# Graph attention on all rows of each head: scores, maxima, exponentials and sums on 128 partitions; logits one step later

## The chip, the cores and the metric

The kernel is one program on one NeuronCore of a Trainium2 chip. The metric is the device time of one execution in microseconds, the median over several runs. "One chunk" below is 512 edges. Engines are named as the profile names them: PE (TensorE), DVE (VectorE), ACT (ScalarE), POOL (GpSimd) and SP (SyncE, which only issues transfers here).

## The reference, cut to what matters

The network takes 100,000 nodes of 64 features and 50,000 edges sorted by destination, and runs four graph layers, each behind a layer norm and a ReLU. Three of the edge passes are attention over the incoming edges of a node, in this form:

```python
z = leaky_relu(xl[src] + xr[dst] + ee, 0.2)          # [E, H, C]
score = einsum('ehc,hc->eh', z, att)                 # one score per edge and head
m = segment_max(score, dst)
a = exp(score - m[dst])
denom = segment_sum(a, dst)
msg = xl[src] * (a / denom[dst])[..., None]
out = segment_sum(msg, dst)
```

Stage a has 8 heads of 16 channels (128 rows), stage b 2 heads of 64 channels (128 rows, and its input has 128 features, so both ends of an edge need a turn of their own), and stage g 4 heads of 16 channels (64 rows). Between b and g stands another layer; its logits are the product of each normalised end of an edge with a weight vector of 64 (`h[src] @ a_src`, `h[dst] @ a_dst`).

## The kernel before, in words

The edges are padded to 98 chunks of 512. `gat_block` is written once and called for stages a, b and g; `R` is the number of feature rows, `H` the number of heads, `wide` is true for b alone. Each engine has its own program, a software pipeline made by `flow` (line 114): a list of stages, each with the number of steps by which it lags, and in step t a stage that lags by s handles chunk t - s. Within a step an engine does its stages in the order of the list, and semaphores tie the engines together. With `SL` = 4 slots, four chunks can be under way in most buffers. A wait on an engine holds everything behind it.

For one chunk, in the order of the data:

- SP loads the indices of both ends (`indices`, line 679), the edge features (`extras`, 690) and START, a row of 512 numbers that is 0 inside a segment and very negative at its start, copied to `H` partitions (`starts`, 704). In stage a SP also stores the gathered rows (693) and the slots that ACT read out of them (697 and 699), behind a wait for `at`; the index loads of a later chunk stand behind these in its queue.
- POOL gathers the rows with eight indirect transfers of 128 rows each (`gather`, 722).
- DVE and ACT normalise in a and g (`norm`, lines 579 to 603; `normed`, 841); in a, ACT then copies two integers out of the gathered rows (`at`, 849).
- PE turns the chunk so that features lie on partitions (`turn`, 929 and 932), ACT copies it (`turned`, 861 and 862), and PE projects it (`project`, 946 to 951) into `bZ` (both ends and the edge) and `bX` (the source alone).
- ACT and DVE make `zt`, the leaky value (`values` 878, `leaky` 760, 761 and 765), and ACT makes `xl` (869 and 871).
- PE makes the scores: `att1b` and its likes are [R, H], so the scores lie on 8, 2 or 4 partitions (`scores`, 957).
- DVE makes the running maximum of a segment with a scan and the two exponents, the decay (row 0) and the weight (row 1) (`maximum`, 774 to 778), and ACT the exponentials `ex` (885).
- DVE scans the denominator on `H` partitions (`denominator`, 787), reading `ex` twice.
- PE spreads decay and weight from H to R rows by products with the 0/1 matrices `sel8`, `sel2` and `sel4` (`factors`, 964 and 965), into the banks `bF0` and `bF1`.
- DVE multiplies weight by `xl` (`sums`, 794) and scans the numerator (799), reading both factors from those banks.
- PE turns numerator (972) and denominator (977, eight small matmul instructions a chunk) so that edges lie on partitions again (`results`). In b, the denominators share the bank `bF2` with the second turn of a later chunk, so there are waits for each other (`rec` in `turn`, `h` in `results`).
- DVE takes the reciprocal (806) and multiplies (812 and 815, 820, or 823), and ACT stores the rows (889).

The list that sets the order on PE is short enough to quote, with that of DVE in stages a and g:

```python
stages = [(L, project), (L + 1, factors), (L, scores), (L - 1, turn), (L + 1, results)]        # PE
stages = [(L, leaky), (L + 2, quotients), (L + 1, denominator), (L + 1, sums), (L, maximum), (L - 2, norm)]
```

`L` is 3 in a and g and 2 in b, which has no norm.

`logit_block` (line 1247) works on 49 batches of 1024 edges with 3 slots: POOL gathers eight times (1290), DVE adds the base rows (1306) and takes the moments, ACT normalises with 16 instructions (1339), and DVE multiplies (1320, two instructions) and sums (1326). On DVE a step is the logits of batch t - 2 and then the norm of t - 1; on ACT it is the stores of the logits of t - 2 and then the normalising of t - 1.

Stage f (`relation_block`, line 1685) is not touched. Its SP queue holds two broadcasts of 256 KB (`kp`, 1746) and 512 KB (`rl`, 1741) ahead of an index load (1731) for which the gathers (1762) wait.

## Time and profile before

| What | us |
|---|---|
| median of 3 runs | 9635.66 (9634.32 to 9646.82) |
| the profiled execution's own time | 9562.17 |
| its span, first to last instruction | 9560.3 |
| DVE busy, share of the span | 6713.4, 70% |
| PE busy | 5960.4, 62% |
| POOL busy | 4490.4, 47% |
| ACT busy | 2831.8, 30% |
| stage a: first and last norm of a gathered row start | 779.8 and 2216.2 |
| stage b: first and last turn start | 2280.8 and 3707.9 |
| logits stage: first and last addition start | 4532.6 and 5266.8 |
| stage g: first and last addition of base rows start | 6991.2 and 8290.4 |

The stages run one after another, so each has its own limit, and the shares of the whole span say little. The lines of an instruction are those of the listing; names such as `a_xg` are the stage's letter and the buffer. PE's bars are modelled, two passes of an f32 product of 512 columns count as two instructions. "issue" as the end of a wait means that the profile shows nothing that the engine waited for. PEclk is the granted clock of TensorE as a share of 2.4 GHz.

### The profile page before, as it was taken

What the parts mean: (1) busy time and instruction counts of PE and PEld (TensorE: products, weight loads), DVE (VectorE), ACT (ScalarE), POOL (GpSimd) and SP (SyncE); (2) the same over time, 40 slices, a digit from 0 to 9 for tenths busy, and PEclk for the clock granted to TensorE, in tenths of its full rate; (3) what the DMA queues carried; (4) which work ended last, traced back from release to release, by engine and by line L of the source; (5) the groups of instructions that cost most, each with busy time, mean ns of one, the idle gap of its engine ahead of it and who ended that gap; (6) DMA issues with size and microseconds to landing.
All of it is one profiled execution on the core that took longest, in us unless ns stands there. A gap on an engine that the chain in (4) does not pass through costs nothing. (4 is left out here: it accounts for less than half of the span.)

```text
span 9560.3 us, 99896 instructions
## 1 busy us (share of the span) xinstructions
PE 5960.4 (62%) x15032; PEld 2923.7 (31%) x15032; DVE 6713.4 (70%) x20701; ACT 2831.8 (30%) x6861; POOL 4490.4 (47%) x4367
## 2 busy tenths in 40 slices
PE   0006999996999997776000889867869999800000
PEld 0002333332444444664000446723323333300000
DVE  2677888885666665887555898867869999877422
ACT  0002333331111112554333000134434444346300
POOL 1775555554555553554554000055556666313466
PEclk9998555555656665555555897578855555555555
DMA  4002334432222221111333002566633333322222
GB/s 146 1 1 44 56 56 56 56 56 50 47 47 47 46 47 28 36 37 44 85 88 80 5 4 67 150 109 130 128 67 74 72 74 73 81 89 110 79 82 78
DMA packets 937356, 627.70 MB, mean 66 GB/s; under 512 B 649081, under 2 KB 811542, under 8 KB 935760
## 3 DMA queue, kind: packets, MB, share of 16 engines
q1 hardware_dynamic: 580324, 305.65, 12.4%
q0 software_dynamic: 137984, 138.92, 11.8%
q10 hardware_dynamic: 218920, 181.82, 5.8%
q14 instruction: 96, 0.79, 0.0%
q8 instruction: 32, 0.52, 0.0%
HBM read 431.25 MB, written 228.04 MB: 69 GB/s over the span
## 5 line engine op out<-in xcount | busy, mean ns | idle before, releaser
L722 POOL DMA_INDIRECT a_xg<-t_XL,a_ix x784 | 785.5, 1002 | 668.3 <-issue 647.5
L722 POOL DMA_INDIRECT b_xg<-t_H,b_ix x784 | 783.3, 999 | 668.1 <-PE b_bank L932 379.6
L722 POOL DMA_INDIRECT g_xg<-t_D,g_ix x784 | 825.8, 1053 | 527.7 <-issue 227.4
L1762 POOL DMA_INDIRECT f_dg<-t_D,f_ix x392 | 383.9, 979 | 1291.1 <-DMA f_ix<-t_PSRC 1163.7
L1105 POOL DMA_INDIRECT t_RANK<-m_place,m_at x392 | 384.5, 981 | 415.0 <-DMA m_place<-t_POS 307.3
L1290 POOL DMA_INDIRECT l_d<-t_D,l_ix x392 | 370.8, 946 | 401.7 <-DVE l_xs L1306 234.1
L2177 POOL DMA_INDIRECT out<-o_y,o_ix x392 | 386.6, 986 | 230.9 <-issue 198.7
L1380 PE MATMUL pr_prow<-c_ident,pr_col 128*1 128x128 f32 x2 | 0.6, 394 | 786.0 <-DVE pr_col L1398 786.0
L445 POOL DMA_INDIRECT t_XL<-ix_pv,ix_si x392 | 407.9, 1041 | 160.0 <-issue 137.7
L760 DVE TENSOR_TENSOR b_zt<-b_xl,b_bank 128x512 f32<-128x512 f32 x98 | 67.4, 687 | 550.9 <-issue 210.2
L1339 ACT ACTIVATE l_hn<-l_xs,l_sm 128x64 f32<-128x64 f32 x784 | 265.0, 426 | 501.7 <-issue 259.6
L2056 POOL TENSOR_TENSOR n_x<-n_x,c_c 128x1280 f32<-128x1280 f32 (+1 forms) x40 | 158.5, 3964 | 513.4 <-DVE n_y L2086 311.0
L1883 ACT ACTIVATE f_hn<-f_xs,f_bykind 128x64 f32<-128x64 f32 x784 | 265.0, 426 | 293.0 <-DVE f_bykind L1793 230.5
L529 PE MATMUL ix_bk<-c_ident,ix_key 128*128 128x128 f32 x56 | 15.6, 435 | 525.0 <-issue 372.9
L2153 DVE TENSOR_TENSOR o_t<-o_ag,c_k 128x256 f32<-128x256 f32 x98 | 41.7, 425 | 416.0 <-DMA o_x<-t_X 330.7
L2099 ACT ACTIVATE n_h<-n_x,n_sm 128x64 f32<-128x64 f32 (+1 forms) x800 | 269.4, 426 | 196.0 <-DVE n_sm L603 196.0
L841 ACT ACTIVATE a_hn<-a_xg,a_sm 128x64 f32<-128x64 f32 x784 | 270.0, 428 | 152.2 <-DVE a_sm L603 106.2
L841 ACT ACTIVATE g_hn<-g_xg,g_sm 128x64 f32<-128x64 f32 x784 | 269.9, 426 | 65.2 <-DVE g_sm L603 59.8
L1128 PE MATMUL m_pa<-c_wca,m_h 65*128 65x64 f32 x784 | 192.7, 427 | 127.4 <-ACT m_h L1209 83.6
L1459 PE MATMUL pb_sums<-pb_rhs,pb_lhs 128*128 128x392 f32 x784 | 260.6, 496 | 12.6 <-DVE pb_rhs L1450 12.6
L1459 PE MATMUL ps_sums<-ps_rhs,ps_lhs 128*128 128x392 f32 x784 | 261.2, 497 | 8.4 <-DVE ps_rhs L1450 8.4
L861 ACT ACTIVATE b_hT<-b_bank 128x512 f32<-128x512 f32 x98 | 58.5, 597 | 673.2 <-PE b_bank L932 640.2
(439 smaller groups left out, 17014.5 us busy)
## 6 DMA issues: line engine op xcount, KB each, us to landing
t_XL<-in_nodes ACTq DMA_DIRECT2D x10, 2578.1 KB
t_XSD<-a_xg SPq DMA_DIRECT2D x98, 256.0 KB
t_H<-a_oE ACTq DMA_DIRECT2D x98, 256.0 KB
l_xb<-t_XSD SPq DMA_DIRECT2D x49, 512.0 KB
f_rl<-t_REL SPq DMA_DIRECT2D x49, 512.0 KB
g_xb<-t_XSD SPq DMA_DIRECT2D x98, 256.0 KB
n_x<-in_x SPq DMA_DIRECT2D x39, 640.0 KB
out<-n_y ACTq DMA_DIRECT2D x39, 640.0 KB
```

The costliest lines, as they stand in the source:

```text
L445: nc.gpsimd.indirect_dma_start(lp, bass.IndirectOffsetOnAxis(ap=si[k][:, j:j + 1], axis=0), pv[k][:, j:j + 1].bitcast(F32), None, bounds_c ...
L722: nc.gpsimd.indirect_dma_start(xg[k][:, j, i, :], None, table, bass.IndirectOffsetOnAxis(ap=ix[k][:, i, j:j + 1], axis=0)).then_inc(s_g[k] ...
L841: last = f(hn[k][:, g // 2, g % 2, :], xg[k][:, g // 2, g % 2, 0:D], ACT.Relu, bias=sm[:, 5, g:g + 1], scale=sm[:, 4, g:g + 1])
L1105: nc.gpsimd.indirect_dma_start(rank, bass.IndirectOffsetOnAxis(ap=at[k][:, j:j + 1], axis=0), place[k][:, j:j + 1], None).then_inc(s_rank[ ...
L1128: last = nc.tensor.matmul(pa[0][k % 2][:, j, :], h[k][:, j * P:(j + 1) * P], C["wca"][:, :], start=True, stop=True)
L1290: nc.gpsimd.indirect_dma_start(d1[k][:, 0, j, :], None, T["D1"], bass.IndirectOffsetOnAxis(ap=ix[k][:, j:j + 1], axis=0)).then_inc(s_g[k], 16)
L1339: last = nc.scalar.activation(hn[k][:, g % 2, g // 2, :], xs[k][:, g // 2, g % 2, :], ACT.Relu, bias=sm[:, 5, g:g + 1], scale=sm[:, 4, g:g ...
L1459: nc.tensor.matmul(sums[:, :], lhs[c % SL][:, :], rhs[c % SL][:, :], start=(c == 0), stop=(c == EF - 1)).then_inc(s_mm, 1)
L1762: nc.gpsimd.indirect_dma_start(dg[k][:, u, j, :], None, T["D2"], bass.IndirectOffsetOnAxis(ap=ix[k][:, u, j:j + 1], axis=0)).then_inc(s_g[ ...
L1883: last = f(hn[k][:, g // J, g % J, c, :], xs[k][:, g // J, g % J, :], ACT.Relu, bias=by_kind[:, c, 1, g:g + 1], scale=by_kind[:, c, 0, g:g ...
L2099: last = f(h[k][0:np_, g, :], x3[k][0:np_, g, :], ACT.Relu, bias=sm[0:np_, 5, g:g + 1], scale=sm[0:np_, 4, g:g + 1])
L2177: nc.gpsimd.indirect_dma_start(out, bass.IndirectOffsetOnAxis(ap=ix[k][:, j:j + 1], axis=0), y[k][:, j, :], None, bounds_check=N - 1, oob_ ...
```

## The change

In the attention stages the attention vectors become [R, 128] matrices in which the column of a head stands once for each row of the head, so that the scores come out on all 128 partitions. Maxima, exponents and exponentials are then made on 128 partitions, START is loaded to 128 partitions, and the products with the 0/1 matrices, the matrices themselves and the banks `bF0` and `bF1` are gone. In a and b the denominator is scanned on 128 rows and turned with four transposes of 128x128 into a bank of its own (`bD`); four numerator transposes stay. In g (`both`), the rows 64 to 127 of the product's operand stay plain weights, the rows 0 to 63 are multiplied in place, and one scan makes numerators and denominators, which are turned together. The second turn of b has its own bank (`bT2`), and its waits on the shared bank go. In `logit_block` there are four slots, and the logits and their stores lag by 3 steps instead of 2.

```diff
@@ setup_block, POOL
-            for name, w in (("sel8", 16), ("sel2", 64), ("sel4", 16)):
...
@@ gat_block
-        start = [m.sb(f"start{k}", [H, CH]) for k in slots]
+        start = [m.sb(f"start{k}", [P, CH]) for k in slots]
...
-        bT, bZ, bX, bS, bF0, bF1, bF2, bO = (m.ps(f"bank{b}", [P, CH]) for b in range(8))
+        bT, bT2, bZ, bX, bS, bD, bO = (m.ps(f"bank{b}", [P, CH]) for b in range(7))
...
-                sp.dma_start(start[k][:, :], line(T["START"], n, H)).then_inc(s_start[k], 16)
+                sp.dma_start(start[k][:, :], line(T["START"], n, P)).then_inc(s_start[k], 16)
...
             def sums(n, k, q, old):
                 ch4.at(n)
-                dve.wait_ge(S["b"], n + 1)
+                dve.wait_ge(S["ex"], n + 1)
                 dve.wait_ge(S["xl"], n + 1)
-                ch4(v.tensor_tensor(msg[:, :], bF1[0:R, :], xl[k][:, :], ALU.mult))
                 if later(n):
                     dve.wait_ge(S["sum"], n)
+                weighted = ex[k][0:R, 1, :] if both else msg[:, :]
+                ch4(v.tensor_tensor(weighted, ex[k][0:R, 1, :], xl[k][:, :], ALU.mult))
                 if old:
                     dve.wait_ge(S["o"], n - SL + 1)
-                v.tensor_tensor_scan(num[k][:, :], bF0[0:R, :], msg[:, :], num[(k - 1) % SL][:, CH - 1:CH],
-                                     ALU.mult, ALU.add).then_inc(S["sum"], 1)
+                v.tensor_tensor_scan(num[k][:, :], ex[k][:, 0, :], ex[k][:, 1, :] if both else msg[:, :],
+                                     num[(k - 1) % SL][:, CH - 1:CH], ALU.mult, ALU.add).then_inc(S["sum"], 1)
...
-                stages = [(L, leaky), (L + 2, quotients), (L + 1, denominator), (L + 1, sums), (L, maximum), (L - 2, norm)]
+                stages = [(L, leaky), (L + 2, quotients), (L + 1, sums), (L, maximum), (L - 2, norm)]
+                if not both:
+                    stages.insert(2, (L + 1, denominator))
...
             def exponents(n, k, q, old):
...
-                    act.wait_ge(S["b"], n - SL + 1)
-                    act.wait_ge(S["den"], n - SL + 1)
+                    act.wait_ge(S["sum"], n - SL + 1)
+                    if not both:
+                        act.wait_ge(S["den"], n - SL + 1)
...
-                if wide and later(n, 3):
-                    pe.wait_ge(S["rec"], n - 2)
...
-                mm(bS[0:H, :], att[:, :], zt[k][:, :], start=True, stop=True).then_inc(S["s"], 1)
-
-            def factors(n, k, q, old):
-
-                pe.wait_ge(S["ex"], n + 1)
-                if later(n):
-                    pe.wait_ge(S["sum"], n)
-                mm(bF0[0:R, :], sel[:, :], ex[k][:, 0, :], start=True, stop=True)
-                mm(bF1[0:R, :], sel[:, :], ex[k][:, 1, :], start=True, stop=True).then_inc(S["b"], 1)
+                mm(bS[:, :], att[:, :], zt[k][:, :], start=True, stop=True).then_inc(S["s"], 1)
...
                 for j in range(J):
-                    tr(bO[:, j * R:(j + 1) * R], split(num[k][:, :])[:, :, j], C["ident"][0:R, 0:R])
-                if wide:
-
-                    hold(pe, S["pturn"], (S["h"], min(n + 3, NCH) if isinstance(n, int) else n + 3))
-                for j in range(J):
-                    last = mm(bF2[:, j * H:(j + 1) * H], split(den[k][:, :])[:, :, j], C["ident"][0:H, 0:H],
-                              start=True, stop=True)
+                    last = tr(bO[:, j * P:(j + 1) * P], split(num[k][:, :])[:, :, j], C["ident"][:, :])
+                    if not both:
+                        last = tr(bD[:, j * P:(j + 1) * P], split(den[k][:, :])[:, :, j], C["ident"][:, :])
                 last.then_inc(S["o"], 1)
-            stages = [(L, project), (L + 1, factors), (L, scores), (L - 1, turn), (L + 1, results)]
+            stages = [(L, project), (L, scores), (L - 1, turn), (L + 1, results)]
@@ weights_block, DVE
+            for name, heads, again in (("att1", 8, 1), ("att2", 2, 1), ("att3", 4, 2)):
...
+                    v.tensor_copy(C[name + "r"][:, :].rearrange("p (g h c) -> p g h c", g=again, c=width)[:, g, :, :],
+                                  bcast(att[:, :], width))
@@ logit_block
-        SL = 3
+        SL = 4
...
-            flow(dve, [(2, logits), (1, norm)], total=NB, slots=SL)
+            flow(dve, [(3, logits), (1, norm)], total=NB, slots=SL)
...
-            flow(act, [(2, store), (1, normed)], total=NB, slots=SL)
+            flow(act, [(3, store), (1, normed)], total=NB, slots=SL)
```

## Rows read from the trace of the kernel before

**Rows 1.** Windows of a, b, g: length, PE, PEld, DVE, ACT, POOL busy us, PEclk, DMA share, GB/s.

```profile
900.00:2200.00 1300.00, 1219.93 (x2370) 501.54 (x2370) 1044.87 (x3228) 502.98 (x1220) 702.00 (x700) 0.52 0.39 56
2400.00:3600.00 1200.00, 1134.82 (x2576) 528.83 (x2576) 741.35 (x1080) 227.88 (x333) 666.55 (x666) 0.61 0.23 47
7100.00:8200.00 1100.00, 1092.10 (x2178) 421.28 (x2178) 1017.25 (x3166) 470.62 (x1000) 707.57 (x668) 0.50 0.36 74
```

**Rows 2.** Timeline, stage a: start us, us, engine, line, instruction [idle before <-releaser].

```profile
1217.47 1.11 DVE L579 BATCH_NORM_STATS2 a_bn<-a_xg 128x6 f32<-128x64 f32 x8 [3.32 <-DMA a_xg<-t_XL,a_ix]
...
1224.90 0.20 ACT L849 ACTIVATE a_at<-a_xg 128x8 int32<-128x8 int32 x1
...
1229.81 0.37 SPq L679 DMA_DIRECT2D a_ix<-t_DST  x1
...
1233.12 0.94 POOL L722 DMA_INDIRECT a_xg<-t_XL,a_ix  x1 [5.88 <-issue]
...
1246.36 0.73 DVE L579 BATCH_NORM_STATS2 a_bn<-a_xg 128x6 f32<-128x64 f32 x5 [2.05 <-DMA a_xg<-t_XL,a_ix]
```

**Rows 3.** Waits of VectorE in stage a, 900 to 2200: total us, times, longest.

```profile
DVE a_bn L579 <- DMA a_xg<-t_XL,a_ix: 162.5, 77, 3.6
```

**Rows 4.** Timeline, stage b, one cycle.

```profile
2861.93 0.69 DVE L760 TENSOR_TENSOR b_zt<-b_xl,b_bank 128x512 f32<-128x512 f32 x1 [4.94 <-issue]
...
2866.55 1.28 DVE L799 TENSOR_TENSOR_SCAN b_num<-b_bank,b_num,b_msg 128x512 f32<-128x512 f32 x1
...
2868.30 1.08 PE L972 MATMUL b_bank<-c_ident,b_num 128*128 128x128 f32 x4
...
2869.85 1.99 PE L977 MATMUL b_bank<-c_ident,b_den 2*128 2x2 f32 x8 [0.47 <-ACT b_hT L862]
...
2871.77 1.13 PE L949 MATMUL b_bank<-b_hT,c_wr 128*128 128x512 f32 x2
...
2873.29 2.08 PE L951 MATMUL b_bank<-b_hT,c_wl 128*128 128x512 f32 x2
...
2876.12 0.69 DVE L760 TENSOR_TENSOR b_zt<-b_xl,b_bank 128x512 f32<-128x512 f32 x1 [4.93 <-PE b_bank L951]
```

**Rows 5.** Waits of VectorE in stage g, 7100 to 8200, the largest.

```profile
DVE g_zt L765 <- issue: 7.4, 20, 1.6
```

**Rows 6.** Timeline, logits stage, one cycle.

```profile
4813.98 1.29 DVE L1320 TENSOR_TENSOR l_pr<-l_hn,c_wb 128x512 f32<-128x512 f32 x2 [5.64 <-issue]
...
4818.48 0.94 POOL L1290 DMA_INDIRECT l_d<-t_D,l_ix  x1 [5.36 <-DVE l_xs L1306]
...
4828.98 1.29 DVE L1320 TENSOR_TENSOR l_pr<-l_hn,c_wb 128x512 f32<-128x512 f32 x2 [5.62 <-issue]
```

**Rows 7.** Timeline, stages a and g: gathers beside VectorE instructions.

```profile
1223.98 1.26 DVE L787 TENSOR_TENSOR_SCAN a_den<-a_ex,a_den 8x512 f32<-8x512 f32 x1
1224.32 1.68 POOL L722 DMA_INDIRECT a_xg<-t_XL,a_ix  x1 [0.30 <-issue]
...
1225.86 1.28 DVE L799 TENSOR_TENSOR_SCAN a_num<-a_bank,a_num,a_msg 128x512 f32<-128x512 f32 x1
...
1226.30 0.94 POOL L722 DMA_INDIRECT a_xg<-t_XL,a_ix  x1 [0.31 <-issue]
...
8132.46 0.67 DVE L777 TENSOR_TENSOR g_rp<-g_r,g_start 4x512 f32<-4x512 f32 x1
...
8132.53 1.41 POOL L722 DMA_INDIRECT g_xg<-t_D,g_ix  x1 [0.30 <-issue]
```

**Rows 8.** Timeline, stage f: an index load behind two broadcasts.

```profile
6513.47 0.53 SPq L1746 DMA_DIRECT2D f_kp<-t_KEEP  x1
...
6514.27 0.35 SPq L1741 DMA_DIRECT2D f_rl<-t_REL  x1
...
6515.01 0.19 SPq L1731 DMA_DIRECT2D f_ix<-t_PSRC  x1
...
6521.14 0.94 POOL L1762 DMA_INDIRECT f_dg<-t_D,f_ix  x1 [3.75 <-DMA f_ix<-t_PSRC]
```

More of the change, by code:

```diff
@@ L633, in gat_block @@
         xl = [m.sb(f"xl{k}", [R, CH]) for k in slots]
-        r = [m.sb(f"r{k}", [H, CH + 1]) for k in slots]
-        ed = [m.sb(f"ed{k}", [H, 2, CH]) for k in slots]
-        ex = [m.sb(f"ex{k}", [H, 2, CH]) for k in slots]
-        rp = m.sb("rp", [H, CH])
-        den = [m.sb(f"den{k}", [H, CH]) for k in slots]
-        recT = [m.sb(f"recT{k}", [P, J * H]) for k in slots]
+        r = [m.sb(f"r{k}", [P, CH + 1]) for k in slots]
+        ed = [m.sb(f"ed{k}", [P, 2, CH]) for k in slots]
+        ex = [m.sb(f"ex{k}", [P, 2, CH]) for k in slots]
+        rp = m.sb("rp", [P, CH])
+        both = R < P
+        if not both:
+            den = [m.sb(f"den{k}", [P, CH]) for k in slots]
+        recT = [m.sb(f"recT{k}", [P, J, H]) for k in slots]
         msg = m.sb("msg", [R, CH])
-        num = [m.sb(f"num{k}", [R, CH]) for k in slots]
+        num = [m.sb(f"num{k}", [P, CH]) for k in slots]
         if wide:
@@ L804, in quotients @@
                 dve.wait_ge(S["o"], n + 1)
-                v.reciprocal(recT[k][:, :], bF2[:, 0:J * H]).then_inc(S["rec"], 1)
+                weights = (bO if both else bD)[:, :].rearrange("p (j r) -> p j r", j=J)[:, :, (R if both else 0)::R // H]
+                v.reciprocal(recT[k][:, :, :], weights).then_inc(S["rec"], 1)
                 dve.wait_ge(S["rec"], n + 1)
@@ L860, in turned @@
                 if wide:
-                    f(hT2[k][:, :], bF2[:, :], ACT.Copy)
+                    f(hT2[k][:, :], bT2[:, :], ACT.Copy)
                 f(hT[k][:, :], bT[:, :], ACT.Copy).then_inc(S["h"], 1)
@@ L882, in exponents @@
                 if old:
-                    act.wait_ge(S["b"], n - SL + 1)
-                    act.wait_ge(S["den"], n - SL + 1)
+                    act.wait_ge(S["sum"], n - SL + 1)
+                    if not both:
+                        act.wait_ge(S["den"], n - SL + 1)
                 f(ex[k][:, :, :], ed[k][:, :, :], ACT.Exp).then_inc(S["ex"], 1)
@@ L956, in scores @@
                     hold(pe, S["pturn"], (S["ed"], n))
-                mm(bS[0:H, :], att[:, :], zt[k][:, :], start=True, stop=True).then_inc(S["s"], 1)
-            def factors(n, k, q, old):
-                pe.wait_ge(S["ex"], n + 1)
-                if later(n):
-                    pe.wait_ge(S["sum"], n)
-                mm(bF0[0:R, :], sel[:, :], ex[k][:, 0, :], start=True, stop=True)
-                mm(bF1[0:R, :], sel[:, :], ex[k][:, 1, :], start=True, stop=True).then_inc(S["b"], 1)
+                mm(bS[:, :], att[:, :], zt[k][:, :], start=True, stop=True).then_inc(S["s"], 1)
             def results(n, k, q, old):
-                hold(pe, S["pturn"], (S["sum"], n + 1), (S["den"], n + 1))
+                hold(pe, S["pturn"], (S["sum"], n + 1))
+                if not both:
+                    hold(pe, S["pturn"], (S["den"], n + 1))
                 if later(n):
@@ L1026, in _ @@
             three_parts(nc, ch, wrow, parts, rest)
+            for name, heads, again in (("att1", 8, 1), ("att2", 2, 1), ("att3", 4, 2)):
+                att = C[name + "b"]
+                rows_ = att.shape[0]
+                width = P // (heads * again)
+                for g in range(again):
+                    v.tensor_copy(C[name + "r"][:, :].rearrange("p (g h c) -> p g h c", g=again, c=width)[:, g, :, :],
+                                  bcast(att[:, :], width))
             for q in range(2):
@@ L1317, in logits @@
                 dve.wait_ge(s_hn, n + 1)
+                if later(n):
+                    dve.wait_ge(s_e, n)
                 for i in range(2):
```

44 lines of the change are left out of this document (19 added, 25 removed).

## The prediction

> **What bounds the kernel now.** I read the busy shares of three attention stages first, then one cycle of each in order of time, and asked which wait ends last. The shares mislead: TensorE is busy 94%, 95% and 99% of the stretches of stages a, b and g [rows 1], yet only in two of them would less TensorE work help at once. Each chunk has eight gathers, so their count gives the pitch of a chunk: 700 in 1300 us is 14.86 us in a, 666 in 1200 us is 14.41 us in b, 668 in 1100 us is 13.17 us in g [rows 1].
>
> Stage a turns on a loop over two chunks without TensorE. Norm of a chunk starts at 1217.47, its slots (`at`) are out on ACT at 1225.10, SP stores them and only then loads the indices of the chunk two ahead (DST issued 1229.81), its first gather starts at 1233.12, and the norm that waited for it starts at 1246.36 [rows 2]: 28.9 us here, 2 x 14.86 = 29.7 in the mean. VectorE waited for these gathers 77 times in 87 chunks [rows 3].
>
> Stage b turns on a loop through PE, ACT and VectorE: leaky starts at 2861.93, the numerator scan ends at 2867.83, four transposes (1.08 us) start at 2868.30, the eight small denominator matmuls (1.99 us) wait 0.47 us for ACT and start at 2869.85, projection starts at 2871.77, and leaky of the next chunk at 2876.12 [rows 4]. 14.19 us.
>
> Stage g has both engines full: PE 1092 of 1100 us, and the largest wait on VectorE is 7.4 us in 84 chunks [rows 1, 5]; its 13.17 us are VectorE's instructions with the semaphore steps between them.
>
> The logits stage repeats every 15.00 us and VectorE stands 5.6 us of it waiting for the 16 normalising activations of the same batch; the gathers idle 5.36 us [rows 6].
>
> **The change, part by part.** *Stage g.* VectorE loses the denominator scan: 1.26 us (the same scan lasts that in a [rows 7]); scan and product keep their length, since 4, 8 and 128 rows of one width cost the same (1.26 us on 8 rows, 1.28 on 128 [rows 7]). PE loses two factor products and eight small matmuls and is no longer full. Gathers need 707.57/83.5 = 8.47 us busy plus 8 x 0.30 us steps = 10.9 us a chunk [rows 1], below 13.17 - 1.26 = 11.9, so VectorE stays the bound: -1.26 x 98 = **-123 us**. Ends: -60 if gathers or ACT start to interfere, -123 as VectorE loses no more.
>
> *Stage b.* VectorE keeps every instruction from leaky to numerator scan, 5.90 us. Then, 0.1 us later as a semaphore step, eight 128x128 transposes, 2 x 1.08 = 2.16 us; the turn that stands before them now runs earlier, because the factor products (L964, L965) are gone. The small matmuls' wait for ACT goes with the shared bank, so nothing stands between. Projection to leaky 4.35 us as now. 5.90 + 0.1 + 2.16 + 4.35 = 12.5 against 14.19: -1.68 x 98 = **-165 us**. Scores with 128 weight columns may take 2.08 us, as L951 does; they lie beside VectorE's quotients and scans. The gathers' own 666.55/83.25 + 2.4 = 10.4 us stay below. The unknown is the clock. In this cycle L949 took 1.13 us for its two passes and L951 2.08 [rows 4]; the first ran at the 2.4 GHz level, the second at 1.2; the stretch's granted clock is 0.61, that of g 0.50, the lower level throughout [rows 1]. With both slow the gain is 0.73 us a chunk, -72 us; with both fast 2.63, -258 us. I take today's mix, the nearest row. The exponential's new wait (for the numerator scan four chunks back) is long past when it is reached.
>
> *Stage a.* TensorE's relief is worth nothing on the loop. Two things are added to it. First, message product and numerator scan read SBUF on both sides instead of one PSUM side. A gather that started 0.34 us into the denominator scan (both inputs in SBUF) lasted 1.68 us and ended 0.76 us after the scan did; one that started 0.44 us into the numerator scan (one input in PSUM) took 0.94 us [rows 7]. So a run of D us of such instructions delays the gather that starts s us into it by D - 0.17 - s: for D = 1.26 that is 0.47 us in the mean over a pitch of 1.25 us, for denominator scan plus product (1.92 us) 1.12. The product's result must be waited for before the scan, and in such a gap a waiting gather gets in: one that started 0.07 us into L777 ended 1.41 us later, not after L778 [rows 7]. The numerator scan then holds the next one 0.07 us. Together +0.7 us a group. Second, START grows from 16 KB to 256 KB (128 copies of one line) and stands in SP's queue just ahead of the index loads that the loop waits for. In stage f an index load issued right behind broadcasts of 256 and 512 KB was used 6.13 us after its issue [rows 8], in a 3.31 us after [rows 2]: 2.8 us for 768 KB, 0.93 for 256 KB; bounds 0 (hidden) and 2.8. So (0.7 + 0.93)/2 x 98 = **+80 us**, ends 0 and +230. The same START in b and g meets index loads that are chunks ahead: nothing, and if that cover were gone, 0.9 us a chunk. VectorE's 1044.87 of 1300 us leaves room for the norm to start when data lands.
>
> The Trainium skill ("SBUF — State Buffer", Who interferes with whom) holds that a tensor_tensor with two SBUF inputs takes only the read side of the port shared with GpSimd, and that making descriptors needs the write side. By that rule no gather would be held and the sum loses its lock terms; the trace's 1.68 us is against it.
>
> *Logits.* With the logits a step later, VectorE no longer waits: 15.00 - 5.64 = 9.4 us of its own [rows 6]. Eight gathers at 1.25 us are 10.0 us and become the bound. The product pair (1.29 us) and the sum of gathered and base rows (about as long) each hold a gather 0.5 us: 11.0. (15.00 - 11.0) x 49 = **-196 us**; ends -245 (no hold) and -150 (both full). ACT's two stores of the logits move with them: ACT now waits there for the batch three back, which VectorE does first in its step, ahead of the norm for which ACT would wait in any case: nothing, or 2.6 us of an ACT that is busy 5.4 of 15. A fourth slot costs memory only.
>
> *Small edits at nothing:* six selects on POOL leave the setup, which is bound by its loads, and four short copies come into the weights block. An exponential over 128 rows costs what 8 cost.
>
> Sum: -123 - 165 + 80 - 196 = -404 us, against the profiled execution's 9562 us, which lies 73 us below the median of the runs, 9635.66. I take the difference over: **9232 us**. A measurement here tells about 0.2% (19 us) from no change.
>
> **Rivals.** *Gathers wait for the whole run.* If none slips in before the numerator scan, the run is 3.2 us, 2.4 us of delay instead of 0.47: a gets (1.93 + 0.93)/2 x 98 = +140, b's gathers come to 12.3 us and cost it perhaps 0.3 us a chunk (-135). Sum -314: 9322. For it: den scan and product stand back to back; against: the 1.41 us gather.
>
> *Clock low in b.* PE then waits 2 to 3 us a chunk for leaky and for the scans. At the low level throughout: -311, 9325. The Trainium skill ("TensorE: Matmul & The Clock Gate", What's actually happening) has sustained work release the full clock and idleness take it away, which points here; but g, busy 99%, was granted 0.50 and b, busy 95%, 0.61 [rows 1], so busy share alone doesn't order them.
>
> *Clock high in b.* Full-width score weights replace two-column ones; both projections fast: -497, 9139.
>
> *Locks cost nothing more,* because gathers and such instructions settle into a rhythm that misses them, as most gathers of g and a do now (0.94 us [rows 7]): a 0.93/2 x 98 = +46, logits -245, sum -487: 9149. The Trainium skill's SBUF page, named above, gives the same.
>
> *Slower:* START's 128 copies of one 2 KB line don't spread over the 16 DMA engines. On one of them they would take 16 x 0.93 = 15 us, every second chunk of a would wait for its indices behind them, and a would lose 14/2 x 98 = 690 us more: 9920. It decides from 404/49 = 8.2 us beyond the 0.93 on. Against: stage f's 768 KB broadcast delayed an index load by 2.8 us [rows 8].
>
> **How the numbers follow.** Forecast 0.40, whole run 0.20, clock low 0.12, clock high 0.13, no lock cost 0.08, START on few engines 0.05; 0.02 that new waits eat the gain to within 19 us. Faster is the sum of the first five, 0.93; same 0.02; slower 0.05. The range has to hold these five with the ends of a and b in part: 9139 less 50 and 9325 plus 75, that is 9090 to 9400.
>
> **What would show it.** Right: a's pitch 15 to 16 us with VectorE still waiting for gathers; b's 12.4 to 13.4 with leaky's wait near 3 us; g's 11.9 with no wait on VectorE; logits 10.5 to 11.5 with the wait moved to the gathers' data. Gathers of 2 us beside L794 show the lock. Wrong: pitch of b or g at that of the gathers, a longer than 16.5 us, or a first gather that starts over 5 us after DST's issue.

## The result, and the profile after

The changed kernel took 9493.85 us (median of four, 9466.74 to 9508.54), the kernel before on the same chip 9637.83. The ratio is 0.9846, with the interval 0.9821 to 0.9871: faster by 144 us, or 1.5%. I had forecast 404 less, and the range, 9090 to 9400, doesn't hold it.

Where did the time go? Each stage from the first to the last start of one kind of instruction (the normalisation's statistics in a, l and g, the gathers in b, one tile's in the others), both kernels profiled:

| stage | before, us | after, us | change | forecast |
|---|---|---|---|---|
| a | 1436 | 1553 | +116 | +80 |
| b | 1392 | 1224 | -168 | -165 |
| l (logits) | 736 | 665 | -71 | -196 |
| g | 1300 | 1351 | +51 | -123 |
| m (places), f, o (output), not touched | 714, 691, 576 | 717, 697, 602 | +3, +6, +26 | 0 |

The changes add up to -37 us, not -144: the profiled execution of the kernel before took 9562.17 us, 76 us less than its median, that of the changed kernel 9508.54, and these two differ by 54 us. In which stages the kernel before usually spends the 76 us more isn't known, so each change in the table may be somewhat too small a gain. Even so, two of four terms have gone wrong in a way that no rival told of. The windows of stages a, b, l and g after (columns as in [rows 1]: busy time and count for PE, PEld, DVE, ACT, POOL, then clock, DMA share, GB/s):

```profile
900.00:2200.00 1300.00, 650.92 (x1546) 291.61 (x1544) 973.91 (x3010) 469.72 (x1137) 711.46 (x650) 0.61 0.43 68
2500.00:3500.00 1000.00, 638.77 (x1832) 339.43 (x1831) 714.27 (x1033) 214.06 (x318) 665.80 (x633) 0.71 0.35 74
4560.00:5040.00 480.00, 0.00 (x0) 0.00 (x0) 309.09 (x1338) 189.30 (x560) 278.19 (x284) 0.50 0.57 97
7000.00:8160.00 1160.00, 637.26 (x1178) 248.74 (x1176) 928.95 (x3122) 477.98 (x1010) 674.08 (x674) 0.55 0.42 89
```

TensorE is relieved as said: 637 of 1160 us in g, where it had been 1092 of 1100 [rows 1]. But VectorE, which was to be full in g, is busy 929 of 1160 us, and in l 309 of 480. Nothing is full. What the stage waits for stands in the waits of g (7000 to 8160 us; engine and line, what it waited for, us in total, times, longest):

```profile
PE g_bank L957 <- DVE g_zt L757: 306.4, 43, 14.5
POOL g_xg L713 <- DMA t_HN<-g_hn: 259.7, 53, 12.4
ACT g_hn L842 <- DVE g_sm L592: 194.6, 41, 11.9
```

ACT waits for VectorE's `sm`, up to 12 us; POOL waits for the store of what ACT makes of it, PE for the `zt` that VectorE makes after it. And VectorE isn't busy. The timeline of one such wait (stage g after; start, duration, instruction, idle before it and its releaser):

```profile
7239.38 0.17 DVE L579 TENSOR_TENSOR g_sm<-g_bn 128x8 f32<-128x8 f32 x1
7239.47 0.16 DVE L580 TENSOR_TENSOR g_sm<-g_bn 128x8 f32<-128x8 f32 x1
7239.55 0.16 DVE L581 TENSOR_TENSOR g_sm<-g_bn 128x8 f32<-128x8 f32 x1
...
7240.66 0.17 DVE L582 TENSOR_TENSOR g_sm<-g_sm 128x8 f32<-128x8 f32 x1 [0.95 <-DVE g_sm L581]
...
7241.39 0.18 DVE L584 SCALAR_TENSOR_TENSOR g_sm<-g_sm 128x8 f32<-128x8 f32 x1 [0.56 <-DVE g_sm L582]
7242.14 0.17 DVE L585 TENSOR_SCALAR g_sm<-g_sm 128x8 f32<-128x8 f32 x1 [0.57 <-issue]
...
7242.80 0.70 SPq L670 DMA_DIRECT2D g_ix<-t_PSRC  x1
7243.55 0.17 DVE L586 TENSOR_SCALAR g_sm<-g_sm 128x8 int32<-128x8 int32 x1 [1.24 <-DVE g_sm L585]
...
7244.24 0.70 SPq L670 DMA_DIRECT2D g_ix<-t_PDST  x1
...
7249.29 0.17 DVE L590 SCALAR_TENSOR_TENSOR g_sm<-g_sm 128x8 f32<-128x8 f32 x1 [1.25 <-DVE g_sm L589]
7250.00 0.17 DVE L591 SCALAR_TENSOR_TENSOR g_sm<-g_sm 128x8 f32<-128x8 f32 x1 [0.54 <-issue]
```

The normalisation ends in a chain of 15 small operations (`norm_factors`, L579 to L592), 0.17 us each and about 3.3 us from first to last start when nothing disturbs it. Here ten of them stand idle first, mostly about 0.55 or 1.24 us, and the chain takes 11.9 us. From here on such a step is called a slow step: one of L580 to L592 with over 0.3 us idle ahead. SyncE has them too: the two index issues, normally 0.43 us apart, are 1.44 us apart here, and over 0.65 us apart in 27 of 98 chunks of g. GpSimd issues its gathers all the while at its 1.24 us. After the change g has 194 slow steps (156 us) and l 188 (155 us); before, the counts over the same steps were 23 (22 us) and 15 (13 us). Of these 38, 35 stand in the first chains of the two stages, beside the 40 and 32 gathers that the kernel before issues there in a row. One stretch of that (kernel before, stage g; the chain is L590 to L603 there):

```profile
7021.49 0.94 POOL L722 DMA_INDIRECT g_xg<-t_D,g_ix  x1 [0.30 <-issue]
7021.82 0.17 DVE L598 TENSOR_SCALAR g_sm<-g_sm 128x8 int32<-128x8 int32 x1 [1.22 <-DVE g_sm L597]
7022.74 0.94 POOL L722 DMA_INDIRECT g_xg<-t_D,g_ix  x1 [0.30 <-issue]
7023.22 0.17 DVE L600 TENSOR_TENSOR g_sm<-g_sm 128x8 f32<-128x8 f32 x1 [1.23 <-DVE g_sm L598]
```

ACT suffers likewise in b: 20 of 97 cycles took over 14 us. One of them in the timeline, with a gather beside two scans and a product ahead of it:

```profile
3080.68 1.28 DVE L779 TENSOR_TENSOR_SCAN b_den<-b_ex,b_den 128x512 f32<-128x512 f32 x1
...
3081.88 0.67 DVE L789 TENSOR_TENSOR b_msg<-b_ex,b_xl 128x512 f32<-128x512 f32 x1
3081.89 1.48 POOL L713 DMA_INDIRECT b_xg<-t_H,b_ix  x1 [0.30 <-issue]
...
3086.64 1.13 PE L951 MATMUL b_bank<-b_hT,c_wl 128*128 128x512 f32 x2
...
3087.53 0.35 ACTq L891 DMA_DIRECT2D t_HR<-b_oE  x1
...
3090.25 0.72 SPq L670 DMA_DIRECT2D b_ix<-t_PSRC  x1
...
3091.66 0.70 SPq L670 DMA_DIRECT2D b_ix<-t_PDST  x1
...
3095.96 0.60 ACT L870 ACTIVATE b_xl<-b_bank 128x512 f32<-128x512 f32 x1 [7.59 <-remote]
...
3096.59 0.69 DVE L752 TENSOR_TENSOR b_zt<-b_xl,b_bank 128x512 f32<-128x512 f32 x1 [9.31 <-ACT b_xl L870]
```

The projection ends at 3087.8, and ACT, free since 3088.4, copies it at 3095.96; VectorE waits 9.31 us for that.

Instruction loading doesn't show in the trace. Between 7300 and 7900 us, where g has its slow steps, the queues that moved anything were these three (of the kernel after), and none is the instruction queue (packets, MB, share of 16 engines):

```profile
q1 hardware_dynamic: 26496, 24.84, 17.3%
q0 software_dynamic: 11168, 11.46, 14.4%
q10 hardware_dynamic: 51832, 17.07, 11.2%
```

The Trainium skill (Runtime: NRT & Kernel Launch, Instruction fetch mechanics) says that a taken branch out of the window held on chip forces a fetch by DMA, and a stall. That would have suited loops of four unrolled chunks; the empty instruction queue of these 600 us speaks against it here. Nor is it the profiler: the executions timed beside the profiled one (9508.54) took 9466.74 to 9503.64.

### The profile page after: what moved, and what is told of

Same layout as the page of the kernel before. It is cut to its first block and busy times, and to the rows that moved or that the text cites. A ratio compares the mean times of both kernels' runs of the same rounds, so it can differ in the third digit from the quotient of the medians.

```text
span 9506.5 us, 93606 instructions
## 1 busy us (share of the span) xinstructions
PE 4305.7 (45%) x12288; PEld 2312.1 (24%) x12288; DVE 6611.2 (70%) x20600; ACT 2830.9 (30%) x6861; POOL 4558.2 (48%) x4361
## 5 line engine op out<-in xcount | busy, mean ns | idle before, releaser
L713 POOL DMA_INDIRECT a_xg<-t_XL,a_ix x784 | 854.2, 1090 | 730.8 <-issue 692.4
L713 POOL DMA_INDIRECT g_xg<-t_D,g_ix x784 | 782.4, 998 | 623.4 <-DMA t_HN<-g_hn 285.9
L713 POOL DMA_INDIRECT b_xg<-t_H,b_ix x784 | 818.6, 1044 | 461.2 <-issue 244.0
L957 PE MATMUL a_bank<-a_zt,c_att1r 128*128 128x512 f32 x196 | 200.4, 1126 | 652.6 <-DVE a_zt L757 330.0
L957 PE MATMUL g_bank<-g_zt,c_att3r 64*128 64x512 f32 x196 | 200.0, 1122 | 590.8 <-DVE g_zt L757 379.1
L957 PE MATMUL b_bank<-b_zt,c_att2r 128*128 128x512 f32 x196 | 193.6, 1090 | 333.6 <-DVE b_zt L753 169.9
L568 DVE BATCH_NORM_STATS2 a_bn<-a_xg 128x6 f32<-128x64 f32 x784 | 108.8, 211 | 323.9 <-DMA a_xg<-t_XL,a_ix 323.9
```

The costliest lines, as they stand in the source:

```text
L713: nc.gpsimd.indirect_dma_start(xg[k][:, j, i, :], None, table, bass.IndirectOffsetOnAxis(ap=ix[k][:, i, j:j + 1], axis=0)).then_inc(s_g[k] ...
L957: mm(bS[:, :], att[:, :], zt[k][:, :], start=True, stop=True).then_inc(S["s"], 1)
```

## The experiments

The code lines under each run show the edit, with `...` where lines are left out. Theories at this point: TRAINS, the slow steps come where GpSimd issues gathers without much of a break; START, its 256 KB broadcasts bring them; and for a's loss START against LOCKS. All ratios below are to the kernel before, run on the same chip in the same batch.

**Batch 1: e1 to e4** (kernel before: 9578.44 us there).

e1, the broadcast made narrow:

```
-                sp.dma_start(start[k][:, :], line(T["START"], n, P)).then_inc(s_start[k], 16)
+                w = H if old else P
+                sp.dma_start(start[k][0:w, :], line(T["START"], n, w)).then_inc(s_start[k], 16)
```

> The changed kernel, with START loaded for the rows of the heads alone (8, 2 or 4 rows, 4 to 16 KB) after the first four chunks of a stage; the rows above keep the values of those first loads, so maxima and weights of most rows are wrong. Theory START (the 256 KB load holds up the index loads behind it in stage a, and slows the small operations of the norm in g): the stretch from the second index load to the first gather in a falls from 5.6 back to about 3.3 us, the 2-chunk loop from 32.0 to about 29.9 us, stage a from 1553 to 1450 us; in g no chain of small operations takes over 4 us, and g goes from 1351 to about 1200 us. Time about 9240 us. Theory TRAINS (the small operations are slow where GpSimd issues gathers without a break): a gains the same 100 us, g keeps its chains of 7 to 12 us and stays at 1330 to 1350 us; time about 9390 us. Theory LOCKS (the port between VectorE and GpSimd made a longer): a stays at 1550 us, time about 9490 us.

9238.20 us, ratio 0.9636 (0.9609 to 0.9662). Stage a took 1468 us, where e2, with the changed kernel's attention, took 1572 on the same chip: START is what a lost by, and LOCKS is out as its main cause. g took 1243 us with 68 slow steps, e2's 1252 with 92; l, where nothing was changed, 643 with 149. START isn't what makes steps slow. That the total meets the 9240 us of theory START is chance: the theory had g at 1200 us with no slow chain, and the kernel before was itself 59 us faster in this batch.

e2, the logits loop put back (SL = 3, product two steps later):

```
-            flow(dve, [(3, logits), (1, norm)], total=NB, slots=SL)
+            flow(dve, [(2, logits), (1, norm)], total=NB, slots=SL)
```

> The changed kernel with the logits loop of before (three buffers, product two steps after its chunk). What it tells is the size of that part alone: stage l back at 736 us from 665, time 9494 + 71 = 9565 us, all other stages as they are. If the slow chains of small operations are bound to the denser gathers of l (TRAINS), none are left in l, whose gathers stand idle 5.36 us a chunk; g keeps its own.

9428.91 us, ratio 0.9849 (0.9829 to 0.9870). l took 739 us with 15 slow steps as before the change, as TRAINS has it. But the ratio is that of the whole change: g, untouched between the two, took 1252 us and not 1351. So the number of slow steps wanders from one run or chip to the next, and the 71 us of l can't be read from the total here.

e3, two of eight gathers left out in g and l (the lines of l are shown), so that the kernel computes with old rows in their places:

```
                 for j in range(K):
+                    if old and j % 4 == 1:
+                        continue
```

> The changed kernel, where the stages l and g leave out two of the eight gathers of each chunk after the first four (old rows stay in those places). GpSimd then works 7.5 us a chunk in place of 10. Theory TRAINS: the small operations keep their 0.2 us a step in both stages; l runs at VectorE's own 10.3 us a chunk (about 510 us in place of 665), g at 11.9 us (about 1170 us in place of 1351), time about 9160 us. Theory TRAFFIC (the slow steps come from the bytes moved by START, stores and loads, of which the gathers are 256 KB of about 1.3 MB a chunk): slow chains remain, l over 600 us, g over 1280 us, time over 9370 us. Theory DEPTH (a buffer more and a later product by themselves): as TRAFFIC in l.

9114.76 us, ratio 0.9515 (0.9495 to 0.9535). l took 487 us, g 1184 (pitch 11.9 in chunk after chunk). They have 15 and 16 slow steps, where the full gathers had 149 in l (e1) and 92 in g (e2) on the same chip, and all of them but one stand in a single chain at the start of each stage, where the gathers of the first chunks are still complete and 38 (g) and 44 (l) are issued in a row. START still moved its 256 KB; TRAFFIC and DEPTH are out.

e4, the same with GpSimd writing 1000 numbers a row (0.98 us) in place of each gather left out:

```
+                        nc.gpsimd.iota(busy[j // 4][:, :], [[1, 1000]], base=0, channel_multiplier=0).then_inc(s_busy, 1)
+                        continue
```

> As the kernel with six gathers, and in the place of the two that are left out GpSimd writes 1000 numbers a row into a buffer that nobody reads (about 1 us each), so that it is as busy as with eight. Theory TRAINS by GpSimd's busy time (whatever it does): slow chains as in the changed kernel, l about 660 us, g about 1350 us, time about 9490 us. Theory TRAINS by the gathers' own descriptors and packets (a break in their train is enough): as with six gathers, l about 520 us, g about 1180 us, time about 9180 us.

9183.19 us, ratio 0.9598 (0.9572 to 0.9623). l 522, g 1229 us, again 15 and 16 slow steps. A GpSimd as busy as with eight gathers doesn't make them; two gathers more in their place do. The stages are longer than in e3 by something else, which the timeline of l shows (scratch write and chain):

```profile
4602.35 0.18 DVE L584 SCALAR_TENSOR_TENSOR l_sm<-l_sm 128x16 f32<-128x16 f32 x1
4602.56 1.30 DVE L585 TENSOR_SCALAR l_sm<-l_sm 128x16 f32<-128x16 f32 x1
4602.85 0.98 POOL L1301 IOTA l_busy<- 128x1000 int32 x1
4603.90 0.17 DVE L586 TENSOR_SCALAR l_sm<-l_sm 128x16 int32<-128x16 int32 x1
```

One small `tensor_scalar` beside the scratch write lasts until that ends: 1.30 us long, not idle ahead of it. It is the rule: in g, 79 of the 92 L585 that ran beside a scratch write lasted over 0.4 us, and none of the 88 L584, a `scalar_tensor_tensor`, did. That is what a hold by a running GpSimd instruction looks like, and a slow step looks different.

**Batch 2: e5 to e8** ran on another chip, where the kernel before took 9244.07 us, 394 less.

> The changed kernel as it is, as the yardstick for the others of this batch and to see how steady its slow chains of small operations are. In its first profile 25 of 98 chains in g and 23 of 49 in l took over 3.8 us; with the logits loop of before the same code of g had only 14 of 98 and g took 1252 us in place of 1351. Theory CHANCE (the slow chains come as the gathers' trains happen to lie): again 10 to 30 slow chains in g, g between 1240 and 1360 us, l 640 to 680 us; ratio to the kernel before 0.983 to 0.988. Theory KNOCK-ON (four buffers in l do something to g): g at 1340 to 1360 us once more.

8779.58 us, ratio 0.9496 (0.9481 to 0.9512): 464 us faster, not 144, which neither CHANCE nor KNOCK-ON had. No slow step in g, none in l. The same code, window by window (a, b, l, g):

```profile
900.00:2200.00 1300.00, 641.38 (x1517) 289.22 (x1515) 956.18 (x2958) 461.39 (x1119) 685.77 (x639) 0.60 0.44 66
2500.00:3300.00 800.00, 540.78 (x1592) 290.00 (x1590) 623.30 (x903) 186.57 (x278) 614.80 (x573) 0.74 0.39 82
4330.00:4780.00 450.00, 0.00 (x0) 0.00 (x0) 364.69 (x1559) 222.65 (x660) 333.48 (x331) 0.50 0.94 118
6500.00:7500.00 1000.00, 637.43 (x1176) 249.80 (x1176) 924.68 (x3107) 476.95 (x1008) 696.36 (x683) 0.55 0.50 103
```

And all that VectorE waits for in g between 6500 and 7560 us (what, us in total, times, longest):

```profile
DVE g_zt L757 <- issue: 6.3, 20, 0.4
DVE g_sm L592 <- DVE g_sm L591: 0.4, 2, 0.2
```

That is 6.7 us in 1060: g is VectorE-bound at a pitch of 11.89 us. Nor is a train of gathers enough by itself: here b issues 464 gathers in a row and g 152, with under 0.6 us between one and the next, and no step is slow. SyncE's two index issues are never over 0.65 us apart. Stages: a 1580, b 1094, l 523, g 1154 us, and m, f, o 663, 623, 499, all three below what they took on the first chip in either kernel; why is open, since nothing was changed in them.

e6, START issued ahead of the stores and their waits (the SyncE line of the attention stages):

```
-            flow(sp, [(0, indices), (1, extras), (1, starts)], slots=SL)
+            flow(sp, [(0, indices), (1, starts), (1, extras)], slots=SL)
```

> The changed kernel, where SyncE issues START of a chunk before the stores of the chunk's gathered columns and not after them, so that in stage a it no longer stands right ahead of the index loads of the next chunk. Nothing is left out. Theory START (its 256 KB delay the landing of the index loads in a): the stretch from the second index load to the first gather falls from 5.6 to under 4 us, the 2-chunk loop from 32.0 to 30.0 to 30.8 us, stage a from 1553 to 1450 to 1500 us; time 50 to 100 us below the changed kernel. Rival (START collides with whatever runs at its time, the gathers or the XSD store included): the loop stays at 31.5 to 32.5 us and the time within 20 us.

8645.66 us, ratio 0.9352 (0.9337 to 0.9368): 134 us below e5, a at 1448 us. The timeline of a in e5 (SyncE's issues around the index loads of a chunk, and the first gather that needs them):

```profile
1238.58 0.35 SPq L695 DMA_DIRECT2D a_start<-t_START  x1
...
1239.66 0.36 SPq L670 DMA_DIRECT2D a_ix<-t_SRC  x1
1240.12 0.38 SPq L670 DMA_DIRECT2D a_ix<-t_DST  x1
...
1246.14 0.94 POOL L713 DMA_INDIRECT a_xg<-t_XL,a_ix  x1 [5.59 <-issue]
```

The same in e6:

```profile
1238.68 0.35 SPq L670 DMA_DIRECT2D a_ix<-t_SRC  x1
1239.13 0.38 SPq L670 DMA_DIRECT2D a_ix<-t_DST  x1
...
1239.69 0.33 SPq L695 DMA_DIRECT2D a_start<-t_START  x1
...
1244.24 0.94 POOL L713 DMA_INDIRECT a_xg<-t_XL,a_ix  x1 [4.09 <-issue]
```

6.02 us from the DST issue to the gather behind START, 5.11 ahead of it. The loop over two chunks of [rows 2], in means over the stage, in us, before (from e8, whose attention stages are those of the kernel before) / e5 / e6:

| part of the loop | before | e5 | e6 |
|---|---|---|---|
| norm to `at` out | 7.67 | 7.61 | 7.65 |
| `at` to DST issue | 3.37 | 3.50 | 2.83 |
| DST issue to first gather | 4.92 | 6.23 | 5.13 |
| eight gathers | 10.27 | 10.84 | 10.92 |
| last gather to next norm | 3.47 | 4.42 | 3.33 |
| sum | 29.71 | 32.58 | 29.86 |

e7, a pause of one scratch write (1.0 us) between the fourth and fifth gather in g and l, all eight kept (the lines of l are shown):

```
+                    if old and j == 4:
...
+                        nc.gpsimd.iota(busy[:, :], [[1, 1000]], base=0, channel_multiplier=0).then_inc(s_busy, 1)
```

> The changed kernel, where in g and l GpSimd writes a scratch buffer (1.0 us, nobody reads it) between the fourth and the fifth gather of a chunk; all eight gathers stay. Theory BREAK (a pause within the train lets the small operations run): at most 3 slow chains in either stage, l paced by GpSimd at 11.0 us a chunk (about 545 us), g at 11.9 (about 1180 us), time 150 to 250 us below the changed kernel. Theory RATE (what matters is how many gathers fall in a stretch, 8 in 11.0 us is 0.73 a us, against 0.50 to 0.62 a us in every loop that showed no slow chain): slow chains remain in both, l 620 to 680 us, g 1240 to 1360 us, time within 50 us of the changed kernel.

8812.21 us, ratio 0.9526 (0.9510 to 0.9542), 33 above e5. With no slow steps to remove on this chip it tells nothing of BREAK and RATE.

> The kernel before with the changed kernel's logits loop alone (four buffers, product three steps after its chunk). Both theories: stage l falls from 736 to 650 to 680 us with 15 to 25 slow chains of 49, the other stages stay, time 60 to 85 us below the kernel before. If the slow chains in l needed anything of the attention part (its state, its memory), l would run at 10 to 11 us a chunk and the gain would be about 190 us.

9052.31 us, ratio 0.9786 (0.9770 to 0.9802): the logits loop alone gives 192 us, l takes 537. No slow step, so the expectation of 15 to 25 slow chains is a miss. Its other case, slow chains in l that need the attention part, named the same gain; that isn't shown either, since on this chip the changed kernel has none. The 192 us fit the forecast of 196.

**Batch 3: e9 to e12** (kernel before: 9269.93 us, a third chip).

> The changed kernel a third time, to separate the chip from the code. On the chip of the first result it took 9494 us (before 9636), with 25 and 23 slow chains of small operations in g and l; on the chip of the last batch 8780 (before 9244), with none. Theory CHIP (slow steps of VectorE and SyncE beside trains of gathers belong to some chips; the code only gives them more trains to meet): the gain follows the kernel before: where that takes about 9240 us, the changed one takes 8780 with no slow chain; where it takes 9560 to 9640, the changed one takes 9420 to 9500 with 10 to 30 in g and 20 or more in l. Theory LUCK (it varies from run to run on any chip): a slow kernel before with a fast changed one, or the other way round, or runs of one batch that differ by over 2%.

8803.62 us, ratio 0.9496 (0.9481 to 0.9512), no slow step in g or l, as theory CHIP has it.

> The kernel with START issued before the stores of the gathered columns, again, with nothing left out. It took 1.5% less than the changed kernel in the last batch (stage a 1448 in place of 1580 us). Theory START: the same 120 to 140 us here on either kind of chip, since a has no slow chains. Rival: on a chip with slow steps SyncE's own issues are late, and the gain in a falls under 80 us.

8667.21 us, ratio 0.9351 (0.9335 to 0.9366): 136 us below e9.

> The changed kernel with a pause of 1.0 us on GpSimd between the fourth and fifth gather of a chunk in g and l. Without slow steps it cost 33 us (l 558 us in place of 523). On a chip with slow steps, theory BREAK: at most 3 slow chains in a stage, l about 560 us and g about 1190, time 150 to 250 us below the changed kernel there; theory RATE (gathers in a stretch are what matters, and 8 in 11 us are too many): slow chains remain, time within 60 us of the changed kernel. On a chip without: 25 to 40 us above the changed kernel, which tells nothing of the two.

8836.54 us, ratio 0.9535 (0.9520 to 0.9551): +33 again.

e12, on top of e6 a shorter chain:

```
-LN_OPS = 15
+LN_OPS = 12
...
-    for _ in range(3):
+    for _ in range(2):
         ch(v.tensor_tensor(t1, y, y, ALU.mult))
```

> The kernel with START issued early, and with two Newton steps in place of three in the reciprocal root of every normalisation: 12 small operations a chain, not 15 (the factor is then exact to about 5e-6 and not to the last bit). On a chip without slow steps: 0.6 us less a chunk where VectorE's chain is on the path: g 1154 to 1100 (-59), l is bound by its gathers (0 to -30), a about -30, the two last stages up to -60: 8480 to 8560 us. On a chip with slow steps, if each instruction of the chain is delayed alike (0.7 or 1.4 us a step), a slow chain loses 3 of its up to 12 slow steps, and the gain is 50 to 80 us more than that; if the slow stretch has a length of its own, whatever stands in it, no more than that.

8582.02 us, ratio 0.9260 (0.9244 to 0.9275): 85 us below e10; g 1154 to 1097, the last stage but one 470 to 445, a 1473 to 1436; f went from 619 to 658, which I can't explain and which puts the time 22 us above the range expected. The chain ends less exactly (about 5e-6, by the expectation).

**Batch 4: e13 to e16** (kernel before: 9631.97 us, a fourth chip, a slow one again).

> The changed kernel, as the yardstick of its batch. Theory CHIP: its gain follows the chip again: about 0.950 of the kernel before where that takes under 9300 us and no chain is slow, about 0.985 where that takes over 9550 us, with 10 to 30 slow chains in g and 20 or more in l.

9447.33 us, ratio 0.9814 (0.9786 to 0.9842), g 1324 us with 165 slow steps, l 660 with 161: CHIP once more. Each of the four chips was met in one batch alone, though, and what its other cores did then is not on record; nor is the chip of the first result. So "chip" here can't be told from the circumstances of a batch. What is shown is that the gain goes with the batch, not with the run.

> START issued before the stores of the gathered columns. On a chip without slow steps 134 to 136 us below the changed kernel, as twice before. On one with them, theory START: the same 100 to 140 us, all of it in a; rival: under 80 us, since SyncE's own issues are late there.

9349.93 us, ratio 0.9718 (0.9683 to 0.9752). a takes 1438 in place of 1558 us, as START has it, and the total falls by 97; the rest of the 120 us was lost in stages that weren't touched.

> The pause of 1.0 us in the middle of each train of g and l. On a chip without slow steps +33 us, as twice before. On one with them, BREAK: at most 3 slow chains in a stage, l about 560 and g about 1190 us, 150 to 250 us below the changed kernel; RATE: slow chains remain, within 60 us of it.

9384.18 us, ratio 0.9738 (0.9711 to 0.9766): 63 below e13. The waits of VectorE in l (4550 to 5060):

```profile
DVE l_sm L591 <- DVE l_sm L590: 13.8, 24, 1.2
DVE l_sm L590 <- DVE l_sm L589: 12.7, 23, 1.2
DVE l_sm L589 <- DVE l_sm L591: 8.2, 16, 1.0
```

The slow steps are there: 138 in l, 103 in g, fewer than e13's 161 and 165, but g had anything from 92 to 194 of them without a pause. BREAK is out: a pause of 1.0 us doesn't free the chain. Whether it takes some steps away isn't shown.

> START early and two Newton steps in place of three. On a chip without slow steps 221 us below the changed kernel, as before (85 below START early). On one with them: 50 to 80 us more than that if each instruction of a chain is delayed alike, no more if the slow stretch has a length of its own.

9341.80 us, ratio 0.9690 (0.9663 to 0.9717), 8 us below e14, within their spread. g has 193 slow steps and l 220, against 130 and 178 in e14, although the chains have three operations fewer. What was saved per chain was given back. That is what a slow stretch with a length of its own would do, but it is one pair of runs, and the counts wander as much between runs with the chain of 15: it isn't shown.

The slow steps of L580 to L592, count and idle us, side by side:

| run | chip by kernel before, us | g | l |
|---|---|---|---|
| before | 9638 | 23, 22 | 15, 13 |
| changed | 9638 | 194, 156 | 188, 155 |
| e1 START narrow | 9578 | 68, 52 | 149, 108 |
| e2 logits as before | 9578 | 92, 69 | 15, 15 |
| e3 six gathers | 9578 | 16, 19 | 15, 18 |
| e4 six, GpSimd busy | 9578 | 16, 20 | 15, 17 |
| e13 changed | 9632 | 165, 124 | 161, 115 |
| e14 START early | 9632 | 130, 104 | 178, 144 |
| e15 pause of 1.0 us | 9632 | 103, 79 | 138, 96 |
| e16 START early, shorter chain | 9632 | 193, 166 | 220, 198 |
| e5 to e8 | 9244 | 0 | 0 |
| e9 to e12 | 9270 | 0 | 0 |

**What is shown and what stays open.** Shown: the gathers make the slow steps (e3 against e1 and e2 on the same chip, with e4 to exclude a merely busy GpSimd), and only in some of the batches, each on a chip of its own. Not shown: what on such a chip makes them, and what decides their number. Gathers in a stretch are a rough measure at best: six in l's 9.3 us are 0.65 a us and leave it undisturbed, eight in g's 11.9 us are 0.67 and don't. A longer pause wasn't tried, nor was another number of gathers than six.

## Why the prediction was wrong, point by point

*The reading of what bounds the kernel* held. TensorE was relieved and only b turned on it; on the chips without slow steps g and l did what their own instructions cost. What failed is a step that my text takes without saying so: that VectorE's small operations, undisturbed in the rows of before, stay so when gathers come denser. The line "its 13.17 us are VectorE's instructions with the semaphore steps between them" was carried over unchanged; the slow steps then added 156 us in g and 155 in l. Two hints stood in the trace of before and weren't read: the 35 slow steps at the start of l and g, where the gathers come without a break (shown above; [rows 5] begins at 7100 us, behind them), and the two index issues of SyncE in a, over 0.65 us apart in 24 of 98 chunks. With the same attention code e8 has neither.

*Stage g, -123.* Step: "VectorE stays the bound: -1.26 x 98". Pitch 11.89 us where 11.9 was said, and 1154 us against 1263 (e5 against e8), -109, on a chip without slow steps; +51 on the first, where its bound didn't hold because of them.

*Logits, -196.* Step: gathers as the bound, 11.0 us. e8 measured -192 in all, the pitch in e5 is 10.86 us in the mean, and VectorE waits for the gathers' data (35.8 us between 4330 and 4780, 24 times, in e5). On the first chip 13.82 us and -71: the 155 us of slow steps are more than the missing 125.

*Stage b, -165.* On the first chip -168, and it looks right; it is two errors that cancel. Without slow steps b went from 1364 to 1094, -270. The mis-sized term is the clock, "I take today's mix": the granted clock rose from 0.61 [rows 1] to 0.74, and the median cycle is 11.0 us. The two passes of L951 took under 1.5 us in 86 of 98 chunks of e5 and in none of e8, those of L949 in 60 and in 35; in the mean both products together fell from 3.65 to 2.59 us, 104 us over 98 chunks, as much as was missing. That is the rival *clock high in b* (-258), though L949 isn't fast throughout. On the first chip the clock rose to 0.71, and the 20 cycles of over 14 us, like the one with ACT's 7.59 us above, hold 118 of the 131 us by which b's 97 cycles are longer than in e5. The rule that I set beside the other rival, of idleness taking the clock away (the Trainium skill, TensorE: Matmul & The Clock Gate, What's actually happening), is not what b did: TensorE went from 95% busy to 68% (540.78 of 800 us) and was granted more. Part of that fall is the faster clock itself, under which the same products take less time. What decided the clock no run here tells apart.

*Stage a, +80.* Measured +116 on the first chip, +139 without slow steps. The lock term, +0.7 us a group of gathers, is about right: 10.27 to 10.84 (and 10.28 to 11.02 on the first chip). The numerator scan of a shows the lock best: of the gathers that started within it none of 92 lasted over 1.2 us before, when it read one operand from PSUM, and 87 of 94 did after, 1.60 us in the median, when it read both from SBUF. Others take 0.94. START's term is mis-sized. I had 0.93 us on the index loads; they cost 1.3 (4.92 to 6.23). And I left out that START runs beside the last gathers, from which to the next norm it now takes 0.95 us more (3.47 to 4.42). e6 takes both back, at next to no price elsewhere (l 531 us against 523): with START loaded early, a takes 1448 us against 1441 before the change. So the rule of the Trainium skill (SBUF — State Buffer, Who interferes with whom), by which no gather would be held, has the trace against it here too.

*START in b and g at nothing* is not contradicted: e1 took 1217 us for b, e2, with the broadcast, 1201 on the same chip, and g differs by 9 us.

*The rivals.* None had the mechanism. "Slower: START on one DMA engine" is out: the index loads were delayed by 1.3 us, not 15.

*The sum.* On the two chips without slow steps 464 and 466 us were gained against 404 forecast. I was 105 too cautious in b and too hopeful by 59 in a, 14 in g and 4 in l; that makes 28 of the 60. The other 32 lie mostly in the ends of the stages, which these marks leave out: from first to last instruction b went from 1445 to 1155 us (-290, not -270), g from 1314 to 1193 (-121) and a from 1492 to 1623 (+131), and l took 15 us less in e5 than in e8. On the first chip the slow steps took back some 320 of it: the changed kernel spends more there than on the second chip in b (130 us), l (142) and g (197), and the kernel before only 28 and 37 in b and g (in a profiled execution that was 76 us faster than its median).

## What to carry to other kernels

Removing the bound of one engine makes the gathers denser, and what a denser train of gathers does to the others must be asked like any other cost: on the first chip some 320 of the 464 us of gain were lost with it. The start of a stage, where gathers already come in a row, is the place in the old trace to look. A gain that comes out at a third of its working on one chip should be measured on a second before its cause is looked for in the code: the same kernel gave ratios of 0.985 and 0.950 here. A large broadcast belongs behind the small load that a loop waits for, and ahead of the waits that would drop it on the gathers: moving one entry of SyncE's order gave 97 to 136 us on each of the three chips it was tried on, and with the shorter chain the best kernel of the study took 0.926 of the time before (0.969 on a chip with slow steps).

## What the runs showed of the hardware

- In the first measurement and in two of the four batches after it, each batch on a chip of its own, instructions of VectorE, SyncE and ACT started about 0.55 or 1.24 us late while GpSimd issued eight gathers a chunk at 1.24 us each; a chain of 15 such instructions took up to 22 us in place of 3.5. With two of eight gathers left out, 149 such steps became 15 in l and 92 became 16 in g. In the two other batches no such step occurred in g and l, even beside 152 gathers in a row, and the kernel before was 3 to 4% faster.
- In 600 us of g with such stretches nothing moved on the instruction queue; the timed executions were as long as the profiled one, within 0.5%.
- A `tensor_scalar` of 16 columns beside a GpSimd write of 1000 columns took 1.30 us in place of 0.17, and ended with it (79 of 92 like it in g lasted over 0.4 us), while none of 88 `scalar_tensor_tensor` was held: such a hold shows as a long instruction, a slow step as idle time ahead of a short one.
- A gather that started within a 128x512 scan with both operands in SBUF took 1.60 us in the median (87 of 94 over 1.2 us), and 0.94 us with one operand in PSUM (none of 92).
- A 256 KB broadcast issued just ahead of a 2 KB index load delayed the first use of the index by 1.3 us (4.92 to 6.23); issued behind it, it did so by 0.2 (5.13).
- In b the granted clock rose from 0.61 to 0.71 (first chip) and 0.74 (e5) as TensorE's busy share fell from 95% to 64 and 68%.
